# Swapping which operands of TensorE stand on whole lines of 128 bytes in a post-norm attention and expert kernel

## The chip, the cores and the metric

The kernel runs on one core of one Trainium2 chip. The metric is device time in microseconds; the kernel before was run three times (median 1031.19 us), and one more execution was taken with the profiler.

## The reference

One post-norm layer on x of 8 batches x 1024 tokens x 256 channels, all fp32. First an attention without softmax, in which the squared and normalised q and k are used:

```python
qkv = x @ Wqkv + bqkv                      # q, k, v of 256 channels each
q = q - mean(q); k = k - mean(k)           # over the channels
q2 = q*q / (sum(q*q) + EPS_SUM); q2 = l2norm(q2, axis=-1)
k2 = k*k / (sum(k*k) + EPS_SUM); k2 = l2norm(k2, axis=-2)
kv = einsum('bnc,bnd->bcd', k2, v)
attn = (v + einsum('bnc,bcd->bnd', q2, kv) / sqrt(N)) @ Wln + bln
x = layernorm(x + attn)
```

Then 16 experts of width 128, every one computed for every token and weighted by its gate:

```python
sel = sigmoid(einsum('bsd,ed->bse', x, expert_sel))
scores = relu(einsum('bsd,edh->bseh', x, keys))
x = layernorm(x + einsum('bseh,ehv,bse->bsv', scores, values, sel))
```

## The kernel before, in words

**Precision.** Every large product is made with fp32r operands split into a high and a low half, name_h and name_l. The helper `product` (line 1204 on) issues three matmuls for each pair of operands: high x high, high x low, low x high. The first operand of `mm` is the stationary one, loaded into the array by a weight load of its own (PEld in the profile); the second is the moving one, streamed through it. The profile names them in the order out<-moving,stationary. The load of the next matmul runs beside the stream of the current one.

**Staging.** The loop runs over 8 batches of 32 steps (two groups of 512 tokens, 16 experts each). In each step TensorE makes:
- the up product of an expert: six matmuls of 512 columns; keys stationary, x1T (x after the attention, transposed) moving; into up_bank;
- what the table `LOOP["plan"]` puts in this step for the attention of the next batch or of the later half (function `layer1`): QK (x^T stationary, wqk moving, 512 columns), GG (x stationary, k2 moving), KS (column sums of k2 against ones), KV (gT, which shares k2's buffer, stationary, wvl moving), QT and XT (transposes: q2 or x1 stationary, the identity moving), Y (x^T stationary and wvl moving, then qT stationary and kvw moving), LG (logits: the selector esel stationary, x1T moving, 512 columns);
- the down product of the expert of the step before: twelve matmuls of 256 columns; gated stationary, vals moving; into down_bank.

wvl is Wv @ Wln, made once. ScalarE and VectorE split, gate and normalise beside it; GpSimd spreads the gates over the partitions; all loads and stores are issued by SyncE. The work of a first batch, without the loop, stands in `first_batch` of each engine and ends at about 47 us.

**Buffers.** `sb` (line 114) takes a buffer of SBUF behind the one before, in the order of the calls. All large buffers are whole multiples of 128 bytes per partition. `half_line` is a buffer of 64 bytes that nothing uses: whatever is allocated ahead of it begins at an address that leaves rest 0 when divided by 128, and what comes behind it begins at rest 64. Every slice that a matmul takes begins a multiple of 512 bytes into its buffer, so it has its buffer's rest. Before the change these are, for the buffers that TensorE reads:

| rest 0 | rest 64 |
|---|---|
| vals, x1T, wqk, wvl, kvw, k2 (also gT), ident, ones | keys, gated, xT, x, qT, esel, and all behind them: q2, x1, the column totals |

Of the kernel before, what the change touches and what calls it, by code (L numbers as in the profile page):

```python
# [6 lines left out]
F32R = mybir.dt.float32r  # L7
# [4 lines left out]
P = 128  # L12
B, N, C = 8, 1024, 256
E, H = 16, 128
M = C // P
T = N // P
GT = 4
GN = GT * P
G = T // GT
# [92 lines left out]
def build_program(nc, x, xT, wqk, wvT, wln, b_qk, b_v, b_ln, esel, keys, values, ident_in, out):  # L112
    with ExitStack() as ctx:
        def sb(name, shape, dt=F32):
            return ctx.enter_context(nc.sbuf_tensor(name, shape, dt))
# [6 lines left out]


        vals_h, vals_l = sb("vals_h", [P, E, C], F32R), sb("vals_l", [P, E, C], F32R)
        x1T_h, x1T_l = sb("x1T_h", [P, G, M, GN], F32R), sb("x1T_l", [P, G, M, GN], F32R)
        wqk_h, wqk_l = sb("wqk_h", [P, M, 2 * C], F32R), sb("wqk_l", [P, M, 2 * C], F32R)
        wvl_h, wvl_l = sb("wvl_h", [P, M, C], F32R), sb("wvl_l", [P, M, C], F32R)
        kvw_h, kvw_l = sb("kvw_h", [P, M, C], F32R), sb("kvw_l", [P, M, C], F32R)
        k2_h, k2_l = sb("k2_h", [P, 2, C], F32R), sb("k2_l", [P, 2, C], F32R)
        gT_h, gT_l = k2_h, k2_l  # L130
        ident, ones = sb("ident", [P, P]), sb("ones", [P, P])


        half_line = sb("half_line", [P, LINE // 8])
        keys_h, keys_l = sb("keys_h", [P, E, M, H], F32R), sb("keys_l", [P, E, M, H], F32R)
        gated_h, gated_l = sb("gated_h", [P, 2, GN], F32R), sb("gated_l", [P, 2, GN], F32R)
        xT_h, xT_l = sb("xT_h", [P, G, M, GN], F32R), sb("xT_l", [P, G, M, GN], F32R)
        x_h, x_l = sb("x_h", [P, 2, C], F32R), sb("x_l", [P, 2, C], F32R)
        qT_h, qT_l = sb("qT_h", [P, 2, 2, M, P], F32R), sb("qT_l", [P, 2, 2, M, P], F32R)
        esel_h, esel_hl = sb("esel_h", [P, M, P], F32R), sb("esel_hl", [P, M, P], F32R)  # L140
        q2, x1 = sb("q2", [P, T, C]), sb("x1", [P, T, C])
        k2_total, k4_total = sb("k2_total", [P, C]), sb("k4_total", [P, C])

# [1398 lines left out]
```

## Time and profile before

| | |
|---|---|
| median of 3 runs | 1031.19 us (1031.14 to 1031.5) |
| profiled execution | 1028.76 us |
| its span, first to last instruction | 1027.0 us |
| TensorE matmul / weight load busy | 98% / 89% |
| VectorE / ScalarE / GpSimd busy | 76% / 48% / 21% |
| DMA, mean | 32 GB/s |

Busy time of matmuls overlaps: a matmul of 256 columns is shown with some 280 ns, but the next one starts well before it ends. To see what a matmul takes of the span, read the distance from its start to the start of the next, over a run of like matmuls.

### The profile page before, as it was taken

The page shows a single profiled execution, that of the slowest core. Times are in us where ns is not written, and L with a number is a line of the kernel's source. Part 1 is how long each engine was busy: PE and PEld are TensorE (multiplying, and loading weights), DVE is VectorE, ACT ScalarE, POOL GpSimd, SP SyncE. Part 2 cuts the span into 40 slices and gives each one's busy share as a digit, 9 for nine tenths or more (in the row PEclk, how much of TensorE's full clock was granted, in tenths as well). Part 3 has the DMA queues.
Part 4 walks back from the last instruction along what each step waited for, and adds up shares of the span by engine and source line. Part 5 has one row for each costly group of instructions (what it writes and reads, how often), then busy time and mean ns, then how long its engine had stood idle before and what let it go on. Part 6 is the DMA issues. An engine that isn't in the chain of part 4 may idle for free.

```text
span 1027.0 us, 18313 instructions
## 1 busy us (share of the span) xinstructions
PE 1008.4 (98%) x6676; PEld 910.8 (89%) x6676; DVE 784.7 (76%) x1790; ACT 497.0 (48%) x1118; POOL 213.1 (21%) x267
## 2 busy tenths in 40 slices
PE   7899999999999999999999999999999999999996
PEld 6788899989989899998999889998899988999886
DVE  5888877878777887777867878687877878777565
ACT  4556633465335653456524565345553465334332
POOL 0021212212122121222122112221222212122221
PEclk9999999999999999999999999999999999999999
DMA  6031001100011000110001100021000200000000
GB/s 183 22 124 62 3 21 43 64 1 3 21 44 62 3 2 21 43 63 2 21 1 54 53 2 22 1 66 39 3 21 6 80 21 3 21 2 23 2 21 21
DMA packets 13469, 32.58 MB, mean 32 GB/s; under 512 B 1858, under 2 KB 3650, under 8 KB 13380
## 3 DMA queue, kind: packets, MB, share of 16 engines
q1 hardware_dynamic: 13380, 31.42, 9.1%
q8 instruction: 53, 0.87, 0.4%
q14 instruction: 36, 0.29, 0.1%
HBM read 22.50 MB, written 8.39 MB: 30 GB/s over the span
## 4 chain that ended last, share of the span: by engine, by line
PE 95%; DVE 3%; issue 1%; ACT 1%; DMA 0%; POOL 0%; DVEq 0%; POOLq 0%
PE up_bank L1210 34%; PE down_bank L1210 33%; PE ring_bank L1210 9%; PE qk_bank L1210 8%; PE g_bank L1210 4%; PE ring_bank L1433 1%; PE ring_bank L1449 1%; PE ring_bank L1456 1%; PE g_bank L1256 1%; PE ring_bank L1455 1%; PE ring_bank L1418 1%; DVE gated_l L980 0%; ACT gated_h L501 0%; DVE gated L974 0%; DMA sel_all<-in_b_qk 0%
## 5 line engine op out<-in xcount | busy, mean ns | idle before, releaser
L501 ACT ACTIVATE gated_h<-gated 128x512 fp32r<-128x512 f32 x256 | 161.5, 631 | 402.1 <-DVE gated L974 402.1
L487 POOL PARTITION_BROADCAST sel_all<-sel_rows x240 | 196.4, 819 | 706.0 <-DVE gated L974 705.2
L1210 PE MATMUL down_bank<-vals_h,gated_h 128*128 128x256 f32 x1024 | 290.5, 284 | 2.3 <-DVE gated_l L980 2.1
L1210 PE MATMUL down_bank<-vals_l,gated_h 128*128 128x256 f32 x1024 | 283.9, 277 | 0.0
L1210 PE MATMUL down_bank<-vals_h,gated_l 128*128 128x256 f32 x1024 | 283.6, 277 | 0.0
L974 DVE SCALAR_TENSOR_TENSOR gated<-up_bank,sel_all 128x512 f32<-128x512 f32 x256 | 175.9, 687 | 63.6 <-PE up_bank L1210 62.1
L980 DVE TENSOR_TENSOR gated_l<-gated,gated_h 128x512 fp32r<-128x512 f32 x256 | 175.2, 684 | 48.6 <-ACT gated_h L501 46.2
L1210 PE MATMUL up_bank<-x1T_h,keys_l 128*128 128x512 f32 x512 | 202.4, 395 | 0.0
L1210 PE MATMUL up_bank<-x1T_l,keys_h 128*128 128x512 f32 x512 | 202.4, 395 | 0.0
L1210 PEld LDWEIGHTS down_bank<-vals_h,gated_h 128*128 128x128 f32 x1024 | 192.4, 188 | 10.9 <-DVE gated_l L980 4.3
L1210 PE MATMUL up_bank<-x1T_h,keys_h 128*128 128x512 f32 x512 | 201.3, 393 | 0.0
L1210 PEld LDWEIGHTS down_bank<-vals_l,gated_h 128*128 128x128 f32 x1024 | 192.8, 188 | 4.8
L1210 PEld LDWEIGHTS down_bank<-vals_h,gated_l 128*128 128x128 f32 x1024 | 192.5, 188 | 0.0
L1210 PEld LDWEIGHTS up_bank<-x1T_h,keys_l 128*128 128x128 f32 x512 | 96.2, 188 | 21.9
L1210 PEld LDWEIGHTS up_bank<-x1T_h,keys_h 128*128 128x128 f32 x512 | 96.2, 188 | 12.2
L1210 PEld LDWEIGHTS up_bank<-x1T_l,keys_h 128*128 128x128 f32 x512 | 96.2, 188 | 11.2
L774 DVE TENSOR_TENSOR qk<-qk_bank,qk_bias 128x512 f32<-128x512 f32 x56 | 38.4, 686 | 33.8 <-PE qk_bank L1210 33.8
L1210 PE MATMUL qk_bank<-wqk_h,xT_h 128*128 128x512 f32 (+1 forms) x128 | 50.3, 393 | 3.4 <-DVE xT_l L1034 1.7
L1210 PE MATMUL qk_bank<-wqk_l,xT_h 128*128 128x512 f32 (+1 forms) x128 | 48.8, 381 | 0.0
L1210 PE MATMUL qk_bank<-wqk_h,xT_l 128*128 128x512 f32 (+1 forms) x128 | 48.7, 381 | 0.0
L792 DVE TENSOR_TENSOR y<-ring_bank,x_raw 128x256 f32<-128x256 f32 x60 | 25.4, 423 | 27.8 <-PE ring_bank L1210 27.8
L501 ACT ACTIVATE k_h<-k,k_scale 128x256 fp32r<-128x256 f32 x56 | 28.6, 510 | 25.3 <-DVE k_scale L826 24.8
(244 smaller groups left out, 1627.5 us busy)
## 6 DMA issues: line engine op xcount, KB each, us to landing
out<-z SPq DMA_DIRECT2D x32, 256.0 KB, 2.4
x_raw<-in_x SPq DMA_DIRECT2D x15, 512.0 KB, 4.7
xT_raw<-in_xT SPq DMA_DIRECT2D x14, 512.0 KB, 3.8
w_room<-in_keys SPq DMA_DIRECT2D x4, 512.0 KB, 3.8
z<-in_values SPq DMA_DIRECT2D x4, 512.0 KB, 3.8
xT_raw<-in_xT SPq DMA_DIRECT2D x4, 256.0 KB, 3.4
sel_rows<-sel SPq DMA_DIRECT2D x64, 8.0 KB
x<-in_wqk SPq DMA_DIRECT2D x2, 256.0 KB, 3.4
```

Of the source, the lines that this page charges most:

```text
L487: nc.gpsimd.partition_broadcast(sel_all[:, e % 2], row, P).then_inc(sel_spread, 1)
L501: return nc.scalar.activation(dst, src, ACT.Copy, **kw)
L774: V.tensor_tensor(qk[:], qk_bank[:], qk_bias[:], ALU.add).then_inc(qk_biased, 1)
L792: V.tensor_tensor(y[:, a % 2], ring_of(it, s, "Y", a)[:, 0:C], x_raw[:, a], ALU.add).then_inc(y_added, 1)
L974: V.scalar_tensor_tensor(out=gated[:], in0=up_bank[s % 2][:], scalar=0.0, in1=sel_all[:, s % 2], op0=ALU.max, op1=ALU.mult).then_inc(gate_ ...
L980: V.tensor_tensor(gated_l[:, s % 2], gated[:], gated_h[:, s % 2].bitcast(F32), ALU.subtract).then_inc(gated_lo, 1)
L1210: last = mm(dst, lhs, rhs, start=start and i == 0, stop=stop and i == n - 1, **kw)
L1256: last = mm(g_bank[:, m * C:(m + 1) * C], x_raw[:, a, m * P:(m + 1) * P], k0_normal[p % 2][:, i], start=(a == 0 and m == 0), stop=(a == T ...
L1418: last = mm(bk[:, j:j + 2], total[:, m * P:(m + 1) * P], ones[:, 0:2], start=True, stop=True)
L1433: last = nc.tensor.transpose(bk[:, j:j + P], q2[:, 2 * a + i, m * P:(m + 1) * P], ident[:])
L1449: last = nc.tensor.transpose(bk[:, m * P:(m + 1) * P], x1[:, a, m * P:(m + 1) * P], ident[:])
L1455: mm(bk[:], esel_hl[:, m], x1T_h[:, a, m], start=(m == 0), stop=False)
```

## The change

Only the order of the buffers is changed. x1T, wqk and wvl now come behind `half_line`; keys, x^T (xT) and the selector (esel) now come ahead of it. kvw, k2, ident, ones and vals stay ahead, gated, x, qT and what follows them stay behind. All code that uses the buffers is the same.

```diff
--- before.py
+++ after.py
@@ -122,22 +122,22 @@
 
 
         vals_h, vals_l = sb("vals_h", [P, E, C], F32R), sb("vals_l", [P, E, C], F32R)
+        keys_h, keys_l = sb("keys_h", [P, E, M, H], F32R), sb("keys_l", [P, E, M, H], F32R)
+        xT_h, xT_l = sb("xT_h", [P, G, M, GN], F32R), sb("xT_l", [P, G, M, GN], F32R)
+        kvw_h, kvw_l = sb("kvw_h", [P, M, C], F32R), sb("kvw_l", [P, M, C], F32R)
+        k2_h, k2_l = sb("k2_h", [P, 2, C], F32R), sb("k2_l", [P, 2, C], F32R)
+        gT_h, gT_l = k2_h, k2_l
+        esel_h, esel_hl = sb("esel_h", [P, M, P], F32R), sb("esel_hl", [P, M, P], F32R)
+        ident, ones = sb("ident", [P, P]), sb("ones", [P, P])
+
+
+        half_line = sb("half_line", [P, LINE // 8])
         x1T_h, x1T_l = sb("x1T_h", [P, G, M, GN], F32R), sb("x1T_l", [P, G, M, GN], F32R)
         wqk_h, wqk_l = sb("wqk_h", [P, M, 2 * C], F32R), sb("wqk_l", [P, M, 2 * C], F32R)
         wvl_h, wvl_l = sb("wvl_h", [P, M, C], F32R), sb("wvl_l", [P, M, C], F32R)
-        kvw_h, kvw_l = sb("kvw_h", [P, M, C], F32R), sb("kvw_l", [P, M, C], F32R)
-        k2_h, k2_l = sb("k2_h", [P, 2, C], F32R), sb("k2_l", [P, 2, C], F32R)
-        gT_h, gT_l = k2_h, k2_l
-        ident, ones = sb("ident", [P, P]), sb("ones", [P, P])
-
-
-        half_line = sb("half_line", [P, LINE // 8])
-        keys_h, keys_l = sb("keys_h", [P, E, M, H], F32R), sb("keys_l", [P, E, M, H], F32R)
         gated_h, gated_l = sb("gated_h", [P, 2, GN], F32R), sb("gated_l", [P, 2, GN], F32R)
-        xT_h, xT_l = sb("xT_h", [P, G, M, GN], F32R), sb("xT_l", [P, G, M, GN], F32R)
         x_h, x_l = sb("x_h", [P, 2, C], F32R), sb("x_l", [P, 2, C], F32R)
         qT_h, qT_l = sb("qT_h", [P, 2, 2, M, P], F32R), sb("qT_l", [P, 2, 2, M, P], F32R)
-        esel_h, esel_hl = sb("esel_h", [P, M, P], F32R), sb("esel_hl", [P, M, P], F32R)
         q2, x1 = sb("q2", [P, T, C]), sb("x1", [P, T, C])
         k2_total, k4_total = sb("k2_total", [P, C]), sb("k4_total", [P, C])
```

The rests after it:

| rest 0 | rest 64 |
|---|---|
| vals, keys, xT, kvw, k2 (also gT), esel, ident, ones | x1T, wqk, wvl, gated, x, qT, q2, x1, the column totals |

## Rows read from the trace of the kernel before

**Rows 1.** The page's span and busy shares, then the core's granted clock; engine, us, share, count.
```profile
span 1027.0 us, 18313 instructions
PE 1008.4 (98%) x6676; PEld 910.8 (89%) x6676; DVE 784.7 (76%) x1790; ACT 497.0 (48%) x1118; POOL 213.1 (21%) x267
...
PEclk9999999999999999999999999999999999999999
...
core 0: 1027.0 us, clock 0.999
```

**Rows 2.** The chain of waits that ended last: shares by engine, then by line.
```profile
PE 95%; DVE 3%; issue 1%; ACT 1%; DMA 0%; POOL 0%; DVEq 0%; POOLq 0%
PE up_bank L1210 34%; PE down_bank L1210 33%; PE ring_bank L1210 9%; PE qk_bank L1210 8%; PE g_bank L1210 4%; PE ring_bank L1433 1%; PE ring_bank L1449 1%; PE ring_bank L1456 1%; PE g_bank L1256 1%; PE ring_bank L1455 1%; PE ring_bank L1418 1%; DVE gated_l L980 0%; ACT gated_h L501 0%; DVE gated L974 0%; DMA sel_all<-in_b_qk 0%
```

**Rows 3.** Waits of TensorE: who waited for whom, total us, times, longest.
```profile
PE down_bank L1210 <- DVE gated_l L980: 2.1, 2, 1.3
```

**Rows 4.** TensorE's groups by form: output<-moving,stationary, shapes, count; busy us, mean ns.
```profile
...
L1210 PE MATMUL down_bank<-vals_h,gated_l 128*128 128x256 f32 x1024 | 283.6, 277 | 0.0
...
L1210 PE MATMUL up_bank<-x1T_h,keys_h 128*128 128x512 f32 x512 | 201.3, 393 | 0.0
L1210 PE MATMUL qk_bank<-wqk_h,xT_h 128*128 128x512 f32 x112 | 45.6, 407 | 0.1
...
L1210 PE MATMUL ring_bank<-wvl_h,xT_h 128*128 128x256 f32 x124 | 34.8, 280 | 0.0
...
L1210 PE MATMUL ring_bank<-wvl_h,k_h 128*128 128x256 f32 x28 | 7.9, 282 | 0.0
```

**Rows 5.** The same of the weight loads.
```profile
L1210 PEld LDWEIGHTS ring_bank<-wvl_h,xT_h 128*128 128x128 f32 x124 | 23.3, 188 | 2.7
...
L1210 PEld LDWEIGHTS ring_bank<-wvl_h,k_h 128*128 128x128 f32 x28 | 5.3, 191 | 0.3
```

**Rows 6.** TensorE in order of time, fast pace: start us, us, line, operation, tiles.
```profile
515.56 0.39 PE L1210 MATMUL up_bank<-x1T_h,keys_h 128*128 128x512 f32 x1
...
516.72 0.40 PE L1210 MATMUL up_bank<-x1T_h,keys_l 128*128 128x512 f32 x1
...
516.96 0.28 PE L1210 MATMUL ring_bank<-wvl_h,xT_h 128*128 128x256 f32 x1
...
517.64 0.28 PE L1210 MATMUL ring_bank<-kvw_h,qT_h 128*128 128x256 f32 x1
...
518.32 0.28 PE L1210 MATMUL down_bank<-vals_h,gated_h 128*128 128x256 f32 x1
...
519.68 0.39 PE L1210 MATMUL up_bank<-x1T_h,keys_h 128*128 128x512 f32 x1
```

**Rows 7.** The same, slow pace, then the product of gT and wvl, then a change of pace.
```profile
506.25 0.28 PE L1210 MATMUL down_bank<-vals_h,gated_h 128*128 128x256 f32 x1
...
507.66 0.39 PE L1210 MATMUL up_bank<-x1T_h,keys_h 128*128 128x512 f32 x1
...
508.82 0.39 PE L1210 MATMUL up_bank<-x1T_h,keys_l 128*128 128x512 f32 x1
...
509.05 0.28 PE L1210 MATMUL ring_bank<-wvl_h,k_h 128*128 128x256 f32 x1
...
510.49 0.60 PE L1433 MATMUL ring_bank<-ident,q 128*128 128x128 f32 x4
...
514.65 0.28 PE L1210 MATMUL down_bank<-vals_l,gated_h 128*128 128x256 f32 x1
...
514.77 0.28 PE L1210 MATMUL down_bank<-vals_h,gated_l 128*128 128x256 f32 x1
...
514.88 0.28 PE L1210 MATMUL down_bank<-vals_h,gated_h 128*128 128x256 f32 x1
```

**Rows 8.** The same in the first batch: fp32 matmuls whose two sides stand at rest 64.
```profile
12.26 1.89 PE L1266 MATMUL down_bank<-x 128*128 128x256 f32 x8
13.99 1.89 PE L1256 MATMUL g_bank<-qk,x_raw 128*128 128x256 f32 x8
```

## The prediction

> **What bounds the kernel now.** I read the busy shares first, then the chain of waits, then the waits of TensorE alone, then its groups by form, and last single matmuls in order of time. TensorE's matmuls are busy 98% of the span, its clock was granted at full level (2.4 GHz) in all 40 slices, and the next engine, VectorE, is at 76% [rows 1]. The chain that ended last is 95% TensorE, 34% in the up product and 33% in the down product [rows 2]. TensorE hardly waits: its longest sum of waits is 2.1 us, on gated_l [rows 3]. So the time is the number of matmuls times the distance between their starts, and only a change of that distance moves it. The change adds and removes no instruction, semaphore or DMA: the 6676 matmuls and 6676 weight loads stay.
>
> Durations in the groups (277 ns for 256 columns) overlap, so I take distances from starts. On the same engine:
> - the six matmuls that stream wvl (rest 0) while x^T (rest 64) is loaded go from 516.96 to 517.64: 0.68 us, 113 ns each; the twelve of a down product (vals 0, gated 64) from 518.32 to 519.68: 1.36 us, 113 ns each [rows 6];
> - another down product with the same buffers takes 506.25 to 507.66: 1.41 us, 117.5 ns each [rows 7]. Down products have these two paces. Followed through the whole timeline, 39 of 255 run at the slow one, in the same places of each batch: behind the column sums and behind some of the transposes. The mean duration agrees: 283.6 us over 1024 is 277.0 ns [rows 4], against 276 at the fast pace and 281 at the slow;
> - the twelve of the product of gT (in k2's buffer) with wvl, here called the kv product, go from 509.05 to 510.49: 1.44 us, 120 ns each [rows 7]. They stream the same wvl at rest 0, but their stationary side k2 stands at rest 0 too. Their weight loads take 191 ns against 188 [rows 5]. This is the one product of the loop in which both sides share a rest;
> - an up product (512 columns) takes 515.56 to 516.96 [rows 6]: 1.40 us, 233 ns each.
>
> So a stream and the load of the next weights do disturb each other, and rests matter: unequal rests 113 ns, equal rests 120 ns for 256 columns.
>
> The Trainium skill says otherwise on loads and streams. Its page SBUF — State Buffer (Who interferes with whom) gives TensorE two independent read ports and says "PE and ACT never wait on anyone", and TensorE: Matmul & The Clock Gate (Back-to-back issue gap) puts a warm matmul at N/2.4 + 2.5 ns. The eight fp32 matmuls of 256 columns at 12.26 to 13.99 us are 216 ns apart [rows 8], what the page gives for a 512-column pass, with both sides at rest 64. The fp32r ones at 113, 120 and 233 ns are not at the page's 109 and 216. By the page's ports the sum would be 0, by these rows it is made with the prices below.
>
> **The change part by part.** Inside a product, the two rests before and after (stream/stationary):
> - up (1536 matmuls), q/k projection (336), the wvl part of Y (372), logits (60) (counts of the first three: three times those in [rows 4]): 0/64 becomes 64/0. Still unequal. No row shows a fp32r stream from rest 64. Bound on one side by the step between unequal and equal rests, 6.6 ns a stream: 2304 x 6.6 = +15.2 us if it always falls on the wrong side. On the other side a gain of the same step, -15.2 us. I take 0, since what the rows tell apart is the difference of the rests, and that stays 64.
> - the kv product (84): 0/0 becomes 64/0. It goes from 1.44 to about 1.36 us, seven times in the loop: -0.6 us. Lower bound of the gain 0.
> - down (3072), q kvw of Y, k2^T x, transposes: rests as before, 0.
>
> What is new lies between products. A load belongs to the next matmul, so at each seam the last stream of one product runs beside the first load of the next. Before, every stream of the loop started at rest 0 and every load but k2's stood at 64, so nearly all seams were unequal. Now the rests are mixed. Following the order in which TensorE is given its work in the loop, seams that turn equal are:
> - 256 columns: down to up 254, wvl to kvw within Y 60, k2^T x to q/k or logits 20, the kv product to transposes 7: 341. At the step to the slow pace (117.5 - 113 = 4.4 ns) that is +1.5 us; at the full step of 6.6 ns +2.3 us; at least 0.
> - 128 columns: 15 transposes before q/k, nothing.
> - 512 columns: up to down, k2^T x, sums or transposes 153, q/k to down or k2^T x 55, logits to down 15: 223. One equal seam of this size stands in the trace, up (rest 0) to the load of the kv product (rest 0): 508.82 to 509.05 is 0.23 us, beside 516.72 to 516.96, 0.24, for an unequal one [rows 6, 7]. I take 0; bounds -5 ns and +6.6 ns each, -1.1 to +1.5 us.
>
> The seams also shift how the load stands against the stream, and this picks the pace of the down product. 122 down products follow an up, q/k or logits product whose last stream now has an equal rest with the first gated load. Slow pace costs 0.05 us a product (1.41 - 1.36). Today 39 of 255 are slow. From the 39 vanishing (-2.0 us) to all 216 others falling in (+10.8 us) is the bound. I take a quarter of the 122, +1.5 us: pace settles mostly back to fast in the rows, since only a minority is slow though transposes and sums upset it each batch.
>
> Sum: +1.5 - 0.6 + 0 + 1.5 = +2.4 us. Cover: ScalarE and VectorE have slack to feed a TensorE that is slower, and their accesses to the moved buffers change only in address. All DMAs keep their place and size. First batch and end (47 us and the last step) hold the same products in small number, nothing. On the profiled execution's own 1028.76 us (span 1027.0 and 1.76 around it) this gives 1031.2. The median of the runs is 1031.19, 2.43 above the profiled execution; the sum is added to the median: 1033.6, rounded 1033.5.
>
> **The rivals.**
> 1. *Slow pace everywhere.* Each seam throws the down product out of its fast pace. For it: the slow pace persists through whole products, as in the one from 506.25 to 507.66 [rows 7]. Against: most upsets heal within a step or two, as at 514.77, where the distance drops from 0.12 to 0.11 in the middle of a product [rows 7]. Most of +10.8 us and the seams: 1036 to 1044, about 1041.
> 2. *The rest itself counts.* A stream that starts half a line in touches one more half on a new line, or a stationary side at rest 0 is what made the kv product slow: its own rests 0/0 cannot tell these from "equal is bad". Price 6.6 ns on 1536 + 336 + 372 + 60 streams, +15.2 us: 1046. If the 512-column streams hide it (their load is done halfway), only 372 x 6.6 = +2.5 us remains: about 1035, within the main case.
> 3. *Nothing.* All seams cost as little as the one at 508.82 [rows 7], the interior is symmetric, and the few kv products stay under what can be told: -0.6 us, 1031. The Trainium skill's rule of independent ports (SBUF — State Buffer, Who interferes with whom) would give the same.
> 4. *Faster.* The seams pull the products out of the slow pace instead: the 39 slow down products become fast (-2.0 us), the kv product gives its 0.6, and the equal 512-column seams are worth -5 ns as the one row hints (-1.1): 1031.2 - 3.7 = 1027.5, about 1028.5 if seams of 256 columns take 1 back. It decides as soon as the seams cost under 0.5 us together. For it: the slow places are fixed by phase, and any shift may free them. Against: nothing in the change aims at what upsets them (sums and transposes, untouched).
>
> **How the numbers follow.** Main case 48%, rivals 12, 13, 12 and 15%. Runs of this kernel can tell about 0.2%, 2.1 us, from no change. The main case spans 1031.3 to 1036.5, so 18 of its 48 points lie within 0.2% and 30 above. Slower: 30 + 12 + 13 = 55%; within: 18 + 12 = 30%; faster: 15%. The range 1029 to 1043 leaves out part of rival 4 (5%), the upper part of rival 1 and the full price of rival 2 (about 13%).
>
> **What would show it.** Equal TensorE counts. The last matmul of a down product before an up one at 117 to 120 ns; the kv product down from 1.44 to 1.36 us; up products still at 1.40 us, and wvl with x^T still at 0.68 us per six. The group means of the down product tell the share of the slow pace: 277 ns now, 281 if all are slow. If up products are longer by 0.04 us (six times 6.6 ns), rival 2 holds. The forecast is wrong if up or wvl products change inside, or if more than a third of the down products change pace.

## The result, and the profile after

The changed kernel takes 1033.3 us (median of 20 runs, 1031.52 to 1035.0) against 1031.16 us of the kernel before beside it (20 runs): ratio 1.0024, 95% interval 1.0018 to 1.0030. It is slower by 2.14 us. (One run of e4_experts_only, below, took 1439.62 us at a granted clock of 0.65 and stays out of its ratio.) One profiled execution of each was taken: before 1028.76 us (span 1027.0), after with a span of 1031.2. These two differ by 4.2 us, more than the medians, so the difference has to be cut up before it is read. The page of after, beside [rows 1, 2]:

```profile
span 1031.2 us, 18313 instructions
PE 1014.0 (98%) x6676; PEld 921.4 (89%) x6676; DVE 786.1 (76%) x1790; ACT 496.9 (48%) x1118; POOL 212.3 (21%) x267
...
PEclk8999999999999999999999999999999999999999
...
PE 95%; DVE 3%; ACT 1%; issue 1%; DMA 0%; POOL 0%; DVEq 0%; POOLq 0%
```

Shares and counts are the same; TensorE is busy 5.6 us longer. One digit of the clock row has changed, the first. The windows, first of before and then of after (stretch, its length, TensorE busy and matmuls, granted clock, DMA share, GB/s):

```profile
8.40:15.20 6.80, 6.25 (x40) 1.00 0.65 197
...
47.00:1010.00 963.00, 960.25 (x6395) 1.00 0.08 28
```

```profile
8.40:15.20 6.80, 5.76 (x26) 0.50 0.60 187
...
47.00:1010.00 963.00, 960.65 (x6369) 1.00 0.08 28
```

From 8.4 to 15.2 us after ran at a granted clock of 0.50, the 1.2 GHz level, and before at the full one; on both sides the engine had been idle for some us just before it (3.28 us in after, 1.73 in before, for xT_l). This belongs to the execution and not to the change: all twelve profiled experiments below have such a stretch too, of 3.4 or 6.8 us, and start their loop at 48.84 to 51.19 us; e1_mirror, whose loop is that of before, starts it at 50.12. The profiled execution of before was the lucky one; at 1028.76 us it also lies below all of its 20 runs (1028.78 and up). It shows in where the loop begins. First matmul of the first up product and last matmul, of before and then of after (start us, us):

```profile
47.62 0.39 PE L1210 MATMUL up_bank<-x1T_h,keys_h 128*128 128x512 f32 x1
...
1019.79 0.28 PE L1210 MATMUL down_bank<-vals_h,gated_l 128*128 128x256 f32 x1
```

```profile
49.35 0.63 PE L1210 MATMUL up_bank<-x1T_h,keys_h 128*128 128x512 f32 x1
...
1024.07 0.28 PE L1210 MATMUL down_bank<-vals_h,gated_l 128*128 128x256 f32 x1
```

So 1.73 us of the 4.25 lie ahead of the loop, and the loop itself went from 972.17 to 974.72 us: +2.55 us, near the +2.14 of the medians. The loop's own start isn't free of the clock either. In after the granted clock was at 0.50 once more, from 49.3 to 52.8 us: that first up product shows 0.63 us a matmul and takes 1.2 us more than six at full clock. In the 5.3 us ahead of it TensorE was busy for 3.4, and in before for 3.6, where the clock stayed up. In before the engine was through early there and then waited 1.3 us for gated_l [rows 3], a wait that after doesn't have. The two nearly make up for each other: from the first down product to the last matmul it is 966.28 and 968.73 us, +2.45. From here on only the loop is read, and one profiled execution gives it to about a microsecond. The groups of after, beside [rows 4, 5] (busy us, mean ns):

```profile
L1210 PE MATMUL down_bank<-vals_h,gated_l 128*128 128x256 f32 x1024 | 285.5, 279 | 0.0
...
L1210 PE MATMUL up_bank<-x1T_h,keys_h 128*128 128x512 f32 x512 | 201.3, 393 | 0.0
L1210 PE MATMUL qk_bank<-wqk_h,xT_h 128*128 128x512 f32 x112 | 45.1, 403 | 0.0
...
L1210 PE MATMUL ring_bank<-wvl_h,xT_h 128*128 128x256 f32 x124 | 34.7, 280 | 0.0
...
L1210 PE MATMUL ring_bank<-wvl_h,k_h 128*128 128x256 f32 x28 | 7.7, 276 | 0.0
```

```profile
L1210 PEld LDWEIGHTS ring_bank<-wvl_h,k_h 128*128 128x128 f32 x28 | 5.3, 188 | 0.3
```

The down product is longer (277 to 279 ns), the kv product shorter (282 to 276), up equal at 393. These means are of overlapping durations, and for up they hide something. In order of time (start us, us):

```profile
248.22 0.39 PE L1210 MATMUL qk_bank<-wqk_h,xT_h 128*128 128x512 f32 x1
...
249.60 0.28 PE L1210 MATMUL down_bank<-vals_h,gated_h 128*128 128x256 f32 x1
...
250.19 0.28 PE L1210 MATMUL down_bank<-vals_h,gated_l 128*128 128x256 f32 x1
...
250.98 0.39 PE L1210 MATMUL up_bank<-x1T_h,keys_h 128*128 128x512 f32 x1
...
252.36 0.28 PE L1210 MATMUL g_bank<-k_h,x_h 128*128 128x256 f32 x1
...
253.06 0.28 PE L1210 MATMUL down_bank<-vals_h,gated_h 128*128 128x256 f32 x1
...
254.42 0.39 PE L1210 MATMUL up_bank<-x1T_h,keys_h 128*128 128x512 f32 x1
...
262.88 0.28 PE L1210 MATMUL ring_bank<-wvl_h,k_h 128*128 128x256 f32 x1
...
264.25 0.38 PE L1433 MATMUL ring_bank<-ident,q 128*128 128x128 f32 x2
```

An up product at 250.98 takes 1.38 us, to the start of the next product at 252.36; before every one took 1.39 or more, as the one of 1.40 in [rows 6]. A down product behind q/k (249.60 to 250.98) takes 1.38 where a fast one took 1.36, and the excess lies in its beginning: its first five distances sum to 0.59 us. The kv product (262.88 to 264.25) is down from 1.44 [rows 7] to 1.37.

For the whole loop I added up the distances from start to start (6453 matmuls; what a distance over 0.4 us has beyond a usual one is set apart as a wait, the slow first up product of after too), by product:

| us in the loop | before | after | difference |
|---|---|---|---|
| down (3072 matmuls) | 357.96 | 362.39 | +4.43 |
| up | 357.19 | 354.50 | -2.69 |
| q/k | 81.09 | 80.33 | -0.76 |
| Y, wvl part | 41.22 | 41.83 | +0.61 |
| Y, kvw part | 40.91 | 42.13 | +1.22 |
| k2^T x | 39.30 | 40.26 | +0.96 |
| kv product | 10.05 | 9.56 | -0.48 |
| down products at the slow pace, of 254 | 40 | 99 | |
| up products under 1.38 us, of 256 | 0 | 145 | |

(Slow is here a mean over 115.5 ns of a product's 6th to 11th distance.) These rows add up to +3.3; logits, transposes, column sums and what was set apart give 0.7 back. So the 2.5 us are what is left of losses of some 7.2 and gains of some 4.7. In the q/k row, after has four matmuls at the lower clock, 0.4 us; without them q/k gained 1.2.

### The profile page after: what moved, and what is told of

It is laid out like the page before. It is cut to its first block, busy times and chain, and to the rows that moved or that the text cites. A ratio compares the mean times of both kernels' runs of the same rounds, so it can differ in the third digit from the quotient of the medians.

```text
span 1031.2 us, 18313 instructions
## 1 busy us (share of the span) xinstructions
PE 1014.0 (98%) x6676; PEld 921.4 (89%) x6676; DVE 786.1 (76%) x1790; ACT 496.9 (48%) x1118; POOL 212.3 (21%) x267
## 4 chain that ended last, share of the span: by engine, by line
PE 95%; DVE 3%; ACT 1%; issue 1%; DMA 0%; POOL 0%; DVEq 0%; POOLq 0%
PE up_bank L1210 34%; PE down_bank L1210 34%; PE ring_bank L1210 9%; PE qk_bank L1210 8%; PE g_bank L1210 4%; PE ring_bank L1433 1%; PE ring_bank L1449 1%; PE ring_bank L1456 1%; PE ring_bank L1455 1%; PE g_bank L1256 1%; PE ring_bank L1418 1%; DVE gated_l L980 0%; ACT gated_h L501 0%; DVE gated L974 0%; DMA sel_all<-in_b_qk 0%
```

## The experiments

Rests modulo 128 turned out not to be enough to tell layouts apart. I use the **distance**: the address of the weights minus that of the stream, modulo 256 bytes. Before it is 64 in every product but the kv product (0). In after it is 192 in up, q/k, the wvl part of Y, logits and kv, and 64 in the rest; the seams down to up and up to down (next weights minus last stream) are both 0. The three numbers hang together: the distance in up is always the sum of the two seams less 64, so moving x1T and keys can't change one of them alone. All kernels in one table; loop sums are of one profiled execution each, the kernel before beside them had medians of 1031.2 to 1031.5:

| kernel | distance in up | seam down-up, up-down | median us | ratio (95%) | down | up | slow down |
|---|---|---|---|---|---|---|---|
| before | 64 | 64, 64 | 1031.16 | | 357.96 | 357.19 | 40 |
| after | 192 | 0, 0 | 1033.3 | 1.0024 (1.0018 to 1.0030) | 362.39 | 354.50 | 99 |
| e1_mirror | 64 | 64, 64 | 1030.55 | 0.9993 (0.9984 to 1.0002) | 358.04 | 357.19 | 41 |
| e3_pad192 | 192 | 192, 192 | 1033.67 | 1.0019 (1.0011 to 1.0028) | 363.44 | 352.79 | 169 |
| e8_pad128 | 128 | 128, 128 | 1046.83 | 1.0156 (1.0142 to 1.0169) | 370.35 | 357.43 | 254 |
| e6_all_equal | 0 | 0, 0 | 1047.02 | 1.0159 (1.0144 to 1.0175) | 372.89 | 355.58 | 254 |
| e4_experts_only | 192 | 0, 0 | 1032.54 | 1.0011 (1.0001 to 1.0020) | 360.74 | 353.84 | 82 |
| e5_attention_only | 64 | 64, 64 | 1035.37 | 1.0036 (1.0024 to 1.0049) | 361.02 | 357.68 | 90 |
| e9_seams_only | 64 | 0, 128 | 1029.9 | 0.9991 (0.9982 to 1.0000) | 357.77 | 356.15 | 25 |
| e11_x64_k128 | 64 | 128, 0 | 1037.49 | 1.0059 (1.0047 to 1.0071) | 363.70 | 357.34 | 135 |
| e7_keys192 | 192 | 192, 64 | 1036.36 | 1.0054 (1.0041 to 1.0066) | 363.60 | 355.18 | 147 |
| e12_x128_k64 | 192 | 64, 192 | 1038.23 | 1.0069 (1.0057 to 1.0081) | 364.69 | 355.41 | 182 |
| e13_x192_k128 | 192 | 128, 128 | 1039.12 | 1.0076 (1.0064 to 1.0088) | 364.72 | 355.36 | 155 |
| e14_streams192 | 64 | 0, 128 | 1031.4 | 0.9998 (0.9989 to 1.0007) | 358.00 | 356.47 | 27 |

**Does the rest itself count, or only the difference?** All buffers moved by 64 bytes, so that every rest changes side and no difference changes:

```diff
+        front_pad = sb("front_pad", [P, LINE // 8])
         vals_h, vals_l = sb("vals_h", [P, E, C], F32R), sb("vals_l", [P, E, C], F32R)
```

> The kernel before with one more unused buffer of 64 bytes ahead of all others: every buffer moves by half a line, so everything that stood at rest 0 stands at 64 and the other way round; all pairs and all seams stay as unequal as before. Theory 1 (only the difference of the rests counts, and the change costs by its seams, where a stream and the next load have equal rests): same as before, 1031 us, up products 1.395 us, down products 1.36 us with about 39 of 255 slow. Theory 2 (the rest itself counts: a stream from 64 with weights at 0 is another case than 0 with 64): up products take 1.375 us, as in the changed kernel behind a fast down product, and the time leaves 1031 by more than 2 us, to about 1026 if the down products stay fast.

```profile
L1211 PE MATMUL down_bank<-vals_h,gated_l 128*128 128x256 f32 x1024 | 284.0, 277 | 0.0
...
L1211 PE MATMUL up_bank<-x1T_h,keys_h 128*128 128x512 f32 x512 | 201.5, 394 | 0.0
...
L1211 PE MATMUL ring_bank<-wvl_h,k_h 128*128 128x256 f32 x28 | 7.9, 283 | 0.0
```

These are groups of e1_mirror. Its time is that of before, and so are its loop sums to 0.1 us. The rest itself costs nothing; rival 2 falls.

**Does 64 equal 192?** Both are half a line in size; modulo 128 they are one case.

```diff
-        half_line = sb("half_line", [P, LINE // 8])
+        half_line = sb("half_line", [P, 3 * LINE // 8])
```

> The kernel before with the unused buffer made 192 bytes instead of 64: the rests by 128 are as before, but the weights now stand 192 instead of 64 bytes on from the streams, counted by 256. If only the rest by 128 counts, as both theories of this case say: 1031 us and products as before. If the order repeats only every 256 bytes, up products change (1.375 us instead of 1.395 would explain the changed kernel's gain in them), time some 1026 us or more than 1033.

In order of time, an up product of 1.38 us and a slow down product of 1.42 of e3_pad192:

```profile
215.77 0.39 PE L1210 MATMUL up_bank<-x1T_h,keys_h 128*128 128x512 f32 x1
...
217.15 0.39 PE L1210 MATMUL qk_bank<-wqk_h,xT_h 128*128 128x512 f32 x1
...
224.27 0.28 PE L1210 MATMUL down_bank<-vals_h,gated_h 128*128 128x256 f32 x1
...
225.69 0.39 PE L1210 MATMUL up_bank<-x1T_h,keys_h 128*128 128x512 f32 x1
```

They are not equal: up falls by 4.4 us, down rises by 5.5, and the slow down products go from 40 to 169. The median is 2.2 us higher (its profiled execution, at 1031.19 us, was the fastest of its 11). This edit has no equal seam but the seven from up into the kv product, which before has too, yet gives the size and the pattern of after. It isn't after's layout, though: here the down products, too, stand at 192 inside, and in after at 64.

**What is the price of equality?** The same line with `LINE // 4` (all distances 128), and with the line taken out (all 0):

```diff
-        half_line = sb("half_line", [P, LINE // 8])
+        half_line = sb("half_line", [P, LINE // 4])
```

> The unused buffer made 128 bytes: all weights stand 128 bytes on from the streams, so all rests by 128 are equal, but by 256 they are not. If only the rest by 128 counts, this is the same as no unused buffer at all: 256-column matmuls 120 ns apart, down products 1.44 us (+20 us over all), Y and k2^T x +3 us: about 1054. If the order goes by 256, it differs from the kernel without the unused buffer; bounds 1031 to 1054.

```diff
-        half_line = sb("half_line", [P, LINE // 8])
```

> The unused buffer left out: every stream and every weight at rest 0. By the kv product of the kernel before (twelve matmuls in 1.44 us): down products 1.44 us, 255 x 0.075 = +19 us, Y and k2^T x 120 matmuls-of-six x 0.04 + 0.04 x 56 = +7 us, up products at least 1.395: 1055 to 1060. If equal rests cost only in the kv product for another reason: within 3 us of before.

Groups of e6_all_equal, and one down product of it, to the up product behind it:

```profile
L1209 PE MATMUL down_bank<-vals_h,gated_l 128*128 128x256 f32 x1024 | 289.7, 283 | 0.0
...
L1209 PE MATMUL up_bank<-x1T_h,keys_h 128*128 128x512 f32 x512 | 203.1, 397 | 0.0
```

```profile
256.02 0.28 PE L1209 MATMUL down_bank<-vals_h,gated_h 128*128 128x256 f32 x1
...
257.46 0.40 PE L1209 MATMUL up_bank<-x1T_h,keys_h 128*128 128x512 f32 x1
```

All 254 down products are slow, and most take 1.43 or 1.44 us, as the kv product did before; +15 us of down make nearly the whole loss. 0 and 128 cost the same within the intervals, so full equality is modulo 128, while 64 and 192 differ. I had expected 1055 to 1060: the 512-column streams, up and q/k, don't pay (up is even 1.6 us shorter than before).

**The two halves of the change.** Experts only (x1T behind, keys and selector ahead), then attention only (wqk and wvl behind, xT ahead):

```diff
-        x1T_h, x1T_l = sb(...)
+        keys_h, keys_l = sb(...)
+        esel_h, esel_hl = sb(...)
         half_line = sb("half_line", [P, LINE // 8])
+        x1T_h, x1T_l = sb(...)
```

> Half of the change: only x1T, keys and the selector are exchanged; wqk, wvl and x^T stay. Equal seams are down to up (254), up to down, to k2^T x, to sums, to transposes and to the wvl and q/k products' loads (x^T now at 64), logits to down. Seam theory: nearly all of the cost of the change that lies in down products is here (+1.5 to +3 us over before: 1033 to 1034), Y's wvl part keeps 0.68 us unless its entry is upset. The rival (the cost sits in the attention products of the loop): within 0.5 us of before.

```diff
-        wqk_h, wqk_l = sb(...)
-        wvl_h, wvl_l = sb(...)
+        xT_h, xT_l = sb(...)
         half_line = sb("half_line", [P, LINE // 8])
+        wqk_h, wqk_l = sb(...)
+        wvl_h, wvl_l = sb(...)
```

> The other half: only wqk, wvl and x^T are exchanged; x1T, keys, selector stay, so down to up and up to down have unequal rests as before. Equal seams: wvl to kvw 60, q/k to down 48, k2^T x to q/k 14, kv product to transposes 7, up to the q/k and wvl products' first load (x^T at 0) 87. Seam theory: a small part, kv product -0.5 us, sum 0 to +1 us: 1031 to 1032, up products 1.395. If up products still show 1.375 us here, the gain in them has nothing to do with their own rests.

In order of time, e4_experts_only: an up product of 1.38 us, and a down product of 1.36 behind k2^T x:

```profile
213.02 0.39 PE L1210 MATMUL up_bank<-x1T_h,keys_h 128*128 128x512 f32 x1
...
214.40 0.28 PE L1210 MATMUL g_bank<-k_h,x_h 128*128 128x256 f32 x1
...
215.10 0.28 PE L1210 MATMUL down_bank<-vals_h,gated_h 128*128 128x256 f32 x1
...
216.46 0.39 PE L1210 MATMUL up_bank<-x1T_h,keys_h 128*128 128x512 f32 x1
```

The experts' half gives the quick up products (162 of 256) and costs 1.1 us in the median. The attention's half has none of them and costs more, 3.9 us, where I had expected 0 to +1. The two don't add: their loops are 1.5 and 4.8 us over that of before, both together 2.55. The head of a down product (its first six distances; medians) tells behind which product it costs: it is 685 ns before; 706 behind up and 685 behind q/k in e4; 685 behind up and 706 behind q/k in e5; 706 behind both in after. So 21 ns are lost in the product behind a 512-column one that has both an equal seam and a distance of 192 inside. Which of the two it is, these kernels can't tell. e11 below has the equal seam behind up with 64 inside, and its head there is mostly 696 or 697 ns in the fast products, 12 more than before.

**Seams without the interior.** The distance in up stays 64, and only what stands at the seams changes. Bases of x1T and keys in e9: 192 and 0; in e11: 64 and 128.

```diff
+        keys_h, keys_l = sb(...)
+        esel_h, esel_hl = sb(...)
         half_line = sb("half_line", [P, LINE // 8])
+        pad_a = sb("pad_a", [P, 32])
+        x1T_h, x1T_l = sb(...)
+        pad_b = sb("pad_b", [P, 32])
```

> x1T stands at 192 and keys and selector at 0 (256), counted by 256, everything else as before. So inside every product the weights stay 64 bytes on from the stream as before; only the seams are changed: down (0) to the keys' load (0) is equal in all 254 places, and up (192) to the loads at 64 is 128 bytes off. Seam theory: the time rises though no product has other rests inside: down products behind up 1.386 instead of 1.362 us and more of them slow, sum +1 to +4 us: 1032.5 to 1035.5, and up products stay over 1.390 us. Rival (what moved the time were the rests inside the products): 1031.5.

```diff
         half_line = sb("half_line", [P, LINE // 8])
+        x1T_h, x1T_l = sb(...)
+        pad_a = sb("pad_a", [P, 16])
+        keys_h, keys_l = sb(...)
+        esel_h, esel_hl = sb(...)
+        pad_b = sb("pad_b", [P, 48])
```

> x1T at 64, keys and selector at 128, counted by 256, the rest as before: inside the up product the weights stay 64 bytes on, down to up is 128 bytes off, and up to the loads of gated, x, q2, x1, x^T is equal (64 to 64). Theory A (an equal seam costs where a 512-column stream runs beside the first load of a 256-column product: 117, 117, 117, 123, 118 ns instead of 118, 113, ... at its head, 24 ns): down products right behind up 1.386 instead of 1.362 us, k2^T x behind up 0.705 instead of 0.685, some more products slow, loop 972.2 to 974 to 976 us, run 1033 to 1035. Theory B (only the distances inside products count): loop 972, run 1031.

A down product of each, to the product behind the up product that follows; e9 first, then e11:

```profile
225.28 0.28 PE L1212 MATMUL down_bank<-vals_h,gated_h 128*128 128x256 f32 x1
...
226.54 0.28 PE L1212 MATMUL down_bank<-vals_h,gated_l 128*128 128x256 f32 x1
226.65 0.39 PE L1212 MATMUL up_bank<-x1T_h,keys_h 128*128 128x512 f32 x1
...
228.04 0.28 PE L1212 MATMUL g_bank<-k_h,x_h 128*128 128x256 f32 x1
```

```profile
214.97 0.28 PE L1212 MATMUL down_bank<-vals_h,gated_h 128*128 128x256 f32 x1
...
216.27 0.28 PE L1212 MATMUL down_bank<-vals_h,gated_l 128*128 128x256 f32 x1
216.39 0.39 PE L1212 MATMUL up_bank<-x1T_h,keys_h 128*128 128x512 f32 x1
...
217.79 0.39 PE L1212 MATMUL qk_bank<-wqk_h,xT_h 128*128 128x512 f32 x1
```

Both have 254 seams from down to up that are equal modulo 128. In e9 (distance 0) the last distance of the down product, 226.54 to 226.65, is 0.11 us and the product takes 1.37; in e11 (128) it is 0.12 and the product takes 1.42. Means over the loop: 113.7 ns and 119.4, against 114.0 before. e9 is the fastest kernel of all, though its interval just reaches no change; e11 loses 6.2 us. My expectation that e9 would be slower was wrong: a seam of 0 from down to up costs nothing in the matmul beside it, one of 128 nearly the full step of 6.6 ns. Over 254 seams this is 1.4 of e11's 6.2 us; the rest lies in slow products (135 against 40), and since e11 also has an equal seam from up to down where e9 has 128, it can't be given to one of the two.

**The interior without equal seams.** Three layouts with 192 in up: e7 (x1T 0, keys 192), e12 (128, 64), e13 (192, 128).

```diff
         half_line = sb("half_line", [P, LINE // 8])
+        pad_a = sb("pad_a", [P, 32])
         keys_h, keys_l = sb(...)
+        esel_h, esel_hl = sb(...)
+        pad_b = sb("pad_b", [P, 32])
```

> The kernel before with keys and selector 192 instead of 64 bytes on from the streams (counted by 256), and nothing else moved: x1T, vals, wqk, wvl stay at 0, gated, x^T, x, qT at 64. No seam has equal rests. Theory (the distance of weights and stream counts by 256, not by 128; up products are faster at 192, 1.375 instead of 1.395 us; down products keep 1.36 us when their seams are unequal): up products of the loop 357 to 353 us in all, down products 358 to 360, time 1027 to 1029, faster than both kernels. Rival (the quick up product is paid back in the down product, as where all weights were moved to 192 bytes, 363 us): 1031 to 1033.

```diff
         half_line = sb("half_line", [P, LINE // 8])
         keys_h, keys_l = sb(...)
+        esel_h, esel_hl = sb(...)
+        pad_a = sb("pad_a", [P, 16])
+        x1T_h, x1T_l = sb(...)
+        pad_b = sb("pad_b", [P, 48])
```

> x1T at 128, keys and selector at 64, the rest as before: inside the up product the weights are 192 bytes on, as in the changed kernel, but down to up is 64 off and up to gated 192 off, so no seam is equal by 128. With e4 (the same inside, both seams equal) and e7 (the same inside, seams 192 and 64) it tells whether the distance inside brings the slow down products by itself. Theory B (it does): up products 1.375 to 1.385 us, down products 362 us or more in all, run 1034 to 1037. Theory A (equal seams are what the down products pay for): up 353 to 355 us, down 358 to 360, run 1027 to 1029.

```diff
         half_line = sb("half_line", [P, LINE // 8])
+        pad_a = sb("pad_a", [P, 16])
         keys_h, keys_l = sb(...)
+        esel_h, esel_hl = sb(...)
+        pad_c = sb("pad_c", [P, 16])
+        x1T_h, x1T_l = sb(...)
+        pad_b = sb("pad_b", [P, 32])
```

> x1T at 192, keys and selector at 128: inside the up product 192 bytes on, down to up and up to gated both 128 bytes off, which is equal by 128. If equality by 128 decides at seams, this is as e4 (up 354, down 361 us in all, loop 973.6, run 1032.5). If a seam of 128 costs nothing, as the time of e9 suggests for up to down, the down products stay at 358 us with up at 354: run 1028 to 1029.

All three missed what I expected of them on the slow side: 5.2 to 7.9 us over before, with 147 to 182 slow down products, up still 1.8 to 2.0 us shorter. Only 105, 20 and 35 of the 256 up products are under 1.38 us, against 162 in e4, so the gain in up hangs on the seams too. e7 and e12 have no equal seam that before doesn't have. Of the four places of x1T and keys with 192 in up, the seams 0 and 0 of e4 are the cheapest by 3.8 us or more. So the equal seams that I charged to the change are, from down to up, more likely what kept it cheap; the seam from up to down changed with it in each of these layouts, and the two aren't told apart.

**After with its streams at 192.** The padding makes every product's distance 64 again and leaves keys and xT at 0, where the change put them:

```diff
         half_line = sb("half_line", [P, LINE // 8])
+        pad_a = sb("pad_a", [P, 32])
         x1T_h, x1T_l = sb(...)
         wqk_h, wqk_l = sb(...)
         wvl_h, wvl_l = sb(...)
+        pad_b = sb("pad_b", [P, 32])
```

> The changed kernel with x1T, wqk and wvl at 192 instead of 64 bytes (counted by 256); keys, x^T and selector stay at 0. Inside every product the weights are then 64 bytes on from the stream again (the kv product too, 0 against 192), down to up stays equal (0), up and q/k to down and k2^T x are 128 off instead of 0. If the changed kernel pays for its 64, that is for the distance 192 inside the up, q/k and Y products and the equal seams up and q/k to down: down products 357 to 359 us instead of 362.4, up 356, Y's two parts 82 to 83 instead of 84, kv 9.6, loop 970 to 972, run 1028.5 to 1030.5, under both kernels. If it pays for the equal seams down to up, which stay: run 1032 or more.

```profile
L1212 PE MATMUL down_bank<-vals_h,gated_l 128*128 128x256 f32 x1024 | 283.8, 277 | 0.0
...
L1212 PE MATMUL up_bank<-x1T_h,keys_h 128*128 128x512 f32 x512 | 201.7, 394 | 0.0
...
L1212 PE MATMUL ring_bank<-wvl_h,xT_h 128*128 128x256 f32 x124 | 35.0, 282 | 0.0
```

These groups of e14_streams192 have down back at 277 ns. The loss is gone in the median (0.9998, 27 slow down products), though all 254 seams from down to up are still equal. Its profiled execution, the slowest of its 11, has a loop of 973.05 us, 0.9 over before: the two parts of Y still cost 2.0 us more. What after lost therefore came with the distance of 192 or with the equal seams behind up, q/k and the wvl part of Y, both of which this edit takes away, and not with the seam from down to up.

## Why the prediction was right

Direction and size came out (+2.4 us forecast, +2.14 measured), and that close by luck: the terms were off by up to 3.5 us and cancelled. One of the prediction's own signs, "the forecast is wrong if up or wvl products change inside", did come.

**What bounds the kernel: right.** Counts and shares are unchanged; all of the loop's +2.55 us is in the distances between starts.

**Inside the products, taken as 0: wrong.** Up gained 2.7 us and q/k 0.8 (1.2 at equal clock), the two parts of Y lost 1.8 and k2^T x 1.0, though kvw, qT, k2 and x all kept their rests. "What the rows tell apart is the difference of the rests" was right in kind (e1_mirror) and wrong in its modulus: 64/0 against 0/64 is a distance of 192 against 64. e3_pad192 shows that going from 64 to 192 in every product but kv, with no new equal seam, moves up by -4.4 us and down by +5.5. That my own test "up still at 1.40 us" fails in 145 of 256 products is the visible trace of it.

**The kv product, -0.6 us: right.** Measured -0.48, each 1.44 to 1.37 us. Equality in the interior is dear, as e6_all_equal and e8_pad128 show on the whole kernel.

**Seams of 256 columns, +1.5 us: mis-sized.** The last distance of the down products went from 114.0 to 115.5 ns, over 254 seams 0.4 us, not the 1.1 that the same seams were charged with. e9_seams_only has them all and no loss. The other 87 of the 341 seams weren't told apart; those within Y may lie behind the slow products named below.

**Seams of 512 columns, 0: mis-sized.** The one row that I had, 0.23 against 0.24 us, measured the matmul ahead of the seam; the 21 ns lie in the six behind it. 87 fast down products follow an up or q/k product: 1.8 us, a little above the upper bound I had given (+1.5). How much of it is the seam's own isn't shown; at the 12 ns of e11, where the inside stays at 64, it would be 1.0, an estimate. Rival 2 had these streams hide what the load loses, "their load is done halfway"; the loads of the rows are shown with 188 ns [rows 5] of such a product's 233. That these streams don't pay for equality is what e6_all_equal shows all the same.

**Pace of the down product, +1.5 us: right that it falls, wrong in where and why, half the size.** 59 more are slow; at the 0.05 us of the prediction this is 3.0 us, and with the 1.8 of the heads 4.8, against +4.43 measured. But I looked for a quarter of the 122 behind up, q/k and logits, whose seam turns equal. There 23 of 121 are slow (11 before), only 12 more; behind Y, k2^T x and transposes, whose last seam hasn't changed, it is 76 of 133 (29 before), 47 more. So the seam just ahead of the product isn't what decides. Behind Y alone it is 25 of 30 in after, 21 in e5, 10 in e4, and none in before, e9 and e14. e3, e7 and e12, without any new equal seam, have 169, 147 and 182 slow products: new equality isn't needed either.

**The rivals.** Slow pace everywhere didn't come (99 of 254). In e8 and e6 every down product is slow, for 16 us, but there each product is also equal inside, at 119 to 120 ns and not the 117.5 of that rival. The rest itself doesn't count. Nothing, by independent ports, is refuted as a rule: the Trainium skill's page SBUF — State Buffer (Who interferes with whom) has "PE and ACT never wait on anyone", yet the same instructions with other addresses cost 15.8 us (e6_all_equal). Faster came about in e9 alone, by some 1.3 us, at the edge of its interval. "If more than a third of the down products change pace" was one of the signs against the forecast: 59 more of 254 is under it.

**Open.** Why a seam of 0 from down to up is cheap and one of 128 dear; why e7 and e12, with no new equality, have more slow down products than after; what each of the two seams of the up product costs alone, and whether after lost by its distance of 192 or by its equal seams behind up, q/k and wvl. The pace seems to carry over from product to product, so that the price of a seam would depend on what stands around it; no rule of single seams that I tried gives all twelve results.

## What to carry to other kernels

Where TensorE bounds a kernel and issues short matmuls with a new weight load each, try the distance of weights and stream. Here 64 bytes modulo 256 was the best of 0, 64, 128 and 192 set for all products, by 2.2 to 15.8 us. And read the effect from distances between starts, since mean durations hide it. Don't take a layout's price from its parts: of seven placements of keys and x1T the best and the worst differ by 9 us, and halves of one change did not add up. Before a difference of a few us between two profiled executions is explained, take out what lies ahead of the loop, here 1.7 of 4.2 us, most of it from the clock.

## What was not expected of the hardware

- The distance of weights and stream counts modulo 256 bytes: per 256-column matmul of a down product, at 64 mostly 113 ns, at 192 a mixture of 113 and 117.5, at 0 and 128 some 120 and 119. 512-column matmuls can be quicker at 192 (1.38 us a product against 1.40) and don't pay for 0.
- A seam can cost nothing in the matmul beside it and still go with 12 to 21 ns in the six behind it.
- Near the beginning the granted clock was 0.50 for some 6.8 us in one profiled execution and 1.00 in another of the same work; the loop began 1.73 us later there. Thirteen of the fourteen profiled executions have such a stretch.
